# Condition lines straight to the partitions, matmuls half block diagonal, and stores from ScalarE's queue, in a conditioned residual kernel

## The reference

```
def reference(x, itok_B_1_198, L0_cond_weights):   # x (64, 64, 512), weights (200, 64, 64)
    w = weights[conditions]
    return x + einsum('bct,bcd->bdt', x, w)         # float32 throughout
```

## Time and profile before

| | us |
|---|---|
| median of 3 runs (lowest, highest) | 48.42 (48.38, 48.78) |
| the profiled execution's own time | 48.91 |
| its span | 47.0 |
| PE busy in it | 16.9 |
| VectorE busy, ScalarE busy | 13.7, 9.4 |
| bytes moved, mean rate over the span | 17.84 MB, 379 GB/s |

### The profile page before, as it was taken

The page is one execution under the profiler, slowest core; times in us unless marked ns, Lnnn a source line. Parts: engine busy times, 40 slices in busy tenths (PEclk is TensorE's granted clock), DMA queues, the critical chain, the costliest instruction groups (busy, mean ns, idle before and its releaser), DMA issues.

```text
span 47.0 us, 351 instructions
## 1 busy us (share of the span) xinstructions
PE 16.9 (36%) x128; PEld 7.0 (15%) x128; DVE 13.7 (29%) x20; ACT 9.4 (20%) x9; POOL 1.7 (4%) x9
## 2 busy tenths in 40 slices
PE   0000000000000005999999999999980000000000
PEld 0000000000000002232333554544610000000000
DVE  1006100000000893003609559559658000000000
ACT  0730000000000000003408448547647000000000
POOL 4000530000000000000000000000000000000000
PEclk9999999999999999999999999999999955555555
DMA  0679999999999999999999999999999999999800
GB/s 0 111 328 432 425 425 404 439 432 432 446 411 404 439 432 432 418 397 425 439 425 425 404 425 425 439 418 397 425 425 418 404 418 439 418 411 411 341 28 7
DMA packets 2451, 17.84 MB, mean 379 GB/s; under 512 B 274, under 2 KB 274, under 8 KB 274
## 3 DMA queue, kind: packets, MB, share of 16 engines
q1 hardware_dynamic: 2304, 16.78, 86.4%
q0 software_dynamic: 144, 1.05, 5.3%
q10 hardware_dynamic: 2, 0.00, 0.0%
HBM read 9.44 MB, written 8.39 MB: 379 GB/s over the span
## 4 chain that ended last, share of the span: by engine, by line
PE 36%; DMA 22%; issue 9%; DVE 8%; POOL 1%; POOLq 1%
PE product L110 36%; DMA gathered<-weights,table_row 22%; DVE w_all L137 5%; DVE y_sb L142 3%; POOL piece L92 1%; DVE gathered L134 1%; POOLq L29 1%; POOLq L151 0%
## 5 line engine op out<-in xcount | busy, mean ns | idle before, releaser
L110 PE MATMUL product<-x_sb,w_all 64*64 64x512 f32 x128 | 16.9, 691 | 18.1 <-DVE w_all L137 18.1
L86 ACT COPY y_sb<-product 128x1024 f32<-128x1024 f32 x8 | 8.1, 1014 | 25.2 <-PE product L110 25.2
L142 DVE COPY y_sb<-product 128x1024 f32<-128x1024 f32 x8 | 9.8, 1225 | 8.4 <-PE product L110 8.4
L110 PEld LDWEIGHTS product<-x_sb,w_all 64*64 64x64 f32 x128 | 7.0, 204 | 27.3 <-DVE w_all L137 18.1
L134 DVE TENSOR_TENSOR gathered<-gathered,piece 128x64 f32<-128x64 f32 x1 | 0.3, 270 | 10.5 <-DMA gathered<-weights,table_row 10.5
L137 DVE STREAM_TRANSPOSE w_all<-gathered 128x2048 f32<-128x2048 f32 x1 | 2.3, 2311 | 0.0
L86 ACT ACT_TABLE_LOAD x1 | 1.3, 1283 | 1.5 <-DVE condition L117 1.5
L124 DVE STREAM_TRANSPOSE condition_of<-condition 32x32 int32<-32x32 int32 x4 | 0.8, 202 | 2.5 <-DMA condition<-conditions 2.4
L94 POOL DMA_INDIRECT gathered<-weights,table_row x1 | 1.1, 1072 | 3.9 <-DVE table_row L128 3.9
L92 POOL MEMSET piece<- 32x1 f32 x4 | 0.4, 92 | 0.5 <-POOLq L151 0.3
L117 DVE MEMSET condition<- 32x64 int32 x1 | 0.1, 112 | 0.8 <-PEq L151 0.8
## 6 DMA issues: line engine op xcount, KB each, us to landing
x_sb<-x SPq DMA_DIRECT2D x8, 1024.0 KB, 14.2
out<-y_sb SPq DMA_DIRECT2D x8, 1024.0 KB, 7.1
condition<-conditions ACTq DMA_DIRECT2D x1, 0.2 KB
gathered<-weights,table_row POOLq DMA_INDIRECT x1, 10.2
```

The lines of the kernel that those rows point to most:

```text
L86: nc.scalar.copy(y_sb[:, 4 * turn:4 * turn + 2, :], product[turn % SETS][0][:, :, :]).then_inc(moved_by_act, 1)
L110: product_of = nc.tensor.matmul(product[turn % SETS][h][halves(g), j, :], w_all[halves(h), :, n], x_sb[halves(h), n, :], start=True, stop= ...
L142: nc.vector.tensor_copy(y_sb[:, 4 * turn + 2:4 * turn + 4, :], product[turn % SETS][1][:, :, :]).then_inc(moved_by_dve, 1)
```

## The change

- The conditions come as 2x32 lines of 16 integers (64 bytes), the condition first in each and zeros behind it. ScalarE loads them with two DMAs, one for each half of the partitions, and each line goes to two partitions. `condition`, its memset, the four transposes and two semaphores go; `table_row` is computed from the loaded lines.
- Turns 0 to 3 multiply as before, on quarters of the array. For turns 4 to 7 a new tensor `w_diag` holds a 128x128 matrix for each pair, with the two items' weights on the diagonal blocks and zeros beside them. VectorE and GpSimd write the zeros, ScalarE the weights: two copies of 64x256 in each of turns 0 to 3, ahead of its copy of that turn's products. A pair is then one call of 128x128 by 128x512. That is 32 calls and 16 calls, 48 instead of 64.
- ScalarE issues the stores, after its own copy and a wait for VectorE's. SyncE issues only the loads.
- The host arranges the result of the two halves differently.

```
-            for turn in range(TURNS):
-                sp.wait_ge(moved_by_act, turn + 1)
-                sp.wait_ge(moved_by_dve, turn + 1)
-                sp.dma_start(out[:, pairs_of(turn), :], y_sb[:, pairs_of(turn), :]).then_inc(stored, 16)
             sp.wait_ge(stored, 16 * TURNS)

         @block.scalar
-            act.wait_ge(condition_cleared, 1)
-            act.dma_start(condition[0:1, :], conditions).then_inc(condition_loaded, 16)
+            for h in range(PAIR):
+                act.dma_start(condition_of[halves(h), :],
+                              bass.AP(conditions.tensor, h * Q * LINE, [[0, K], [LINE, Q], [1, LINE]])
+                              ).then_inc(condition_loaded, 16)
             for turn in range(TURNS):
+                if turn < TILED:
+                    later = slice(4 * turn, 4 * turn + 4)
+                    act.wait_ge(w_ready, 1)
+                    for h in range(PAIR):
+                        nc.scalar.copy(w_diag[halves(h), later, h * D:(h + 1) * D],
+                                       w_all[halves(h), :, pairs_of(TILED + turn)].rearrange("p d n -> p n d")
+                                       ).then_inc(w_placed, 1)
                 act.wait_ge(multiplied, turn + 1)
                 nc.scalar.copy(y_sb[:, 4 * turn:4 * turn + 2, :], product[turn % SETS][0][:, :, :]
                                ).then_inc(moved_by_act, 1)
+                act.wait_ge(moved_by_act, turn + 1)
+                act.wait_ge(moved_by_dve, turn + 1)
+                act.dma_start(out[:, pairs_of(turn), :], y_sb[:, pairs_of(turn), :]).then_inc(stored, 16)

         @block.gpsimd
+            pool.wait_ge(pieces_set, 2 * (P // Q))
+            nc.gpsimd.memset(w_diag[halves(1), :, 0:D], 0.0).then_inc(w_zeroed, 1)
             pool.wait_ge(rows_known, 1)

         @block.tensor
+                if turn == TILED:
+                    pe.wait_ge(w_zeroed, 2)
+                if turn >= TILED:
+                    pe.wait_ge(w_placed, PAIR * (turn - TILED + 1))
                 for j in range(2):
                     for g in range(2):
+                        n = 4 * turn + 2 * j + g
+                        if turn >= TILED:
+                            product_of = nc.tensor.matmul(product[turn % SETS][j][:, g, :], w_diag[:, n - 4 * TILED, :],
+                                                          x_sb[:, n, :], start=True, stop=True)
+                            continue

         @block.vector
-            nc.vector.memset(condition[:, :], 0).then_inc(condition_cleared, 1)
             for q in range(P // Q):
                 nc.vector.memset(piece[q * Q:(q + 1) * Q, 1:2], float(q % K)).then_inc(pieces_set, 1)
-            dve.wait_ge(condition_loaded, 16)
-            for q in range(P // Q):
-                nc.vector.transpose(condition_of[q * Q:(q + 1) * Q, :], condition[:, q // K:B:PAIR]
-                                    ).then_inc(condition_turned, 1)
+            nc.vector.memset(w_diag[halves(0), :, D:PAIR * D], 0.0).then_inc(w_zeroed, 1)
+            dve.wait_ge(condition_loaded, 16 * PAIR)
             dve.wait_ge(pieces_set, 2 * (P // Q))
-            dve.wait_ge(condition_turned, P // Q)
...
+    conditions = np.zeros((PAIR, B // PAIR, LINE), np.int32)
+    conditions[:, :, 0] = np.asarray(itok_B_1_198).reshape(B // PAIR, PAIR).T
```

More of the change, by code:

```diff
@@ L20, in conditioned_residual_kernel @@
     P, PAIRS, T = x.shape
-    B = conditions.shape[1]
     C = D = P // PAIR
+    LINE = conditions.shape[2]
     Q = 32
@@ L44, in conditioned_residual_kernel @@
         w_all = sbuf("w_all", [P, D, PAIRS], fp32)
+        w_diag = sbuf("w_diag", [P, PAIRS - 4 * TILED, PAIR * D], fp32)
         product = [[ctx.enter_context(nc.psum_tensor(f"product{s}_{h}", [P, 2, T], fp32)) for h in range(PAIR)]
@@ L50, in conditioned_residual_kernel @@
         condition_loaded = semaphore("condition_loaded")
-        condition_cleared = semaphore("condition_cleared")
         pieces_set = semaphore("pieces_set")
-        condition_turned = semaphore("condition_turned")
         rows_known = semaphore("rows_known")
@@ L105, in _ @@
                     pe.wait_ge(moved_by_dve, turn - SETS + 1)
+                if turn == TILED:
+                    pe.wait_ge(w_zeroed, 2)
+                if turn >= TILED:
+                    pe.wait_ge(w_placed, PAIR * (turn - TILED + 1))
                 for j in range(2):
                     for g in range(2):
+                        n = 4 * turn + 2 * j + g
[3 more added lines that the diff above has]
+                            continue
                         for h in range(PAIR):
-                            n = 4 * turn + 2 * j + g
                             product_of = nc.tensor.matmul(product[turn % SETS][h][halves(g), j, :],
```

17 lines of the change are left out of this document (11 added, 6 removed).

## The result

| | before | changed |
|---|---|---|
| median, us (lowest to highest, runs) | 48.6 (48.38 to 49.01, 4) | 60.78 (60.5 to 62.15, 4) |
| profiled execution, its span | 48.91, 47.0 | 60.69, 58.7 |
| PE's start, PE's end, in the span | 18.12, 35.07 | 28.47, 53.15 |

The ratio is 1.244, 95% interval 1.233 to 1.256. The forecast was 64.4 within 56 to 67.5: the right way, and 3.6 us too much.

The account below looks back on a forecast made before the run. The prediction took DMA bytes to bound the kernel before. PE's start at 33.0 plus 30.0 behind it gave a span of 63.0; 1.9 beyond the span, less 0.5 for the median, gave 64.4 us, range 56 to 67.5.

Parts of the forecast that it names:

- The slack: At PE's start: could come 4 to 6 us later at its present pace before compute, not DMA, set the end.
- Two engines: Conditions' DMAs: the source's outermost count of 2 puts each on two engines; bounds one and sixteen.
- 66 packets, each behind a load packet.: Conditions' landing: packets per engine alternate with loads, 66 x 0.275 = 18.2 us from 2.9; wait ends at 22.6.
- From conditions to PE: Conditions' landing to first matmul: gather issued at 23.1, takes 7.2 us, lands at 30.3; PE starts at 33.0.
- Behind PE's start: PE's start to span's end: 30.0 us, with turns 0 to 3 10.1, ScalarE's delay 0.2, turns 4 to 7 13.8.
- Worth nothing: Stores on a queue apart from the loads: no gain, since the loads are over by then.
- From span to time: End of the sum: span 63.0; profiled execution 1.9 beyond its span, 64.9; median 0.5 lower, 64.4 us.
- Weight loads at nothing: PE's turns: weight loads, 16 per turn at a mean of 204 ns, hide behind streaming and cost nothing.
- The first: Rival on conditions' DMA: lines are quick, compute ends late; sixteen engines 51.0 us, or two draining many packets 49.8; chance 0.12.
- The second: Rival on conditions' DMA: each on engines of its own, or four engines; PE at 26.3, time 57.7 us; chance 0.09.
- The fourth: Rival at the start: lines drain in a burst ahead of the loads, table row at 3.3, time 48.1 us; chance 0.05.
- Profile signs: Expected in the profile: 132 small packets over some 19 us, loads landed by 24, DMA idle from 24 to 27.

Follow-up runs that it names:

- (a): Kernel before with only the conditions' lines changed (two DMAs from ScalarE, outermost count 2): 59.02 us against 48.94.
- j_tiled6_more_calls: Kernel before with the last two turns block diagonal, plus 8 small matmul calls ahead of turn 0: 50.00 us against 48.86, ratio 1.042.
- f_tiled6: Kernel before with only the last two turns block diagonal, conditions and stores as before: 47.93 us against 48.86, ratio 0.995.
- (c): Kernel before with only the stores' issue moved from SyncE to ScalarE: 48.90 us against 48.94.
- (k): Changed kernel with only the conditions as before (one line, transposes): 50.61 us against 48.38, ratio 1.045.
- (b): Kernel before with only the half block diagonal matmuls, conditions and stores as before: 49.52 us against 48.94.
- (d): Changed kernel with the conditions written out as 128 lines by the host, one DMA on sixteen engines: 50.85 us against 48.94.
- f_tiled5: Kernel before with only the last three turns block diagonal, conditions and stores as before: 48.20 us against 48.86, ratio 0.993.
- (g): Changed kernel with 128 written-out condition lines on sixteen engines and two block diagonal turns instead of four: 47.90 us against 48.38, ratio 0.989.

## Why the prediction was right, and where it was off

**What bounds the kernel.** That the bytes set the time of before held. The slack did not: PE was to start 4 to 6 us later at its present pace for nothing, but in (a) it starts 10.4 us later at that pace and the time rises by 10.1. The stores on SyncE's queue before, and then the DMA row of the page of (a), a slice being 1.43 us:

```profile
23.22 13.96 SPq L77 DMA_DIRECT2D out<-y_sb  x8
```

```profile
DMA  0799999999999999920000008999999999999910
```

Before, the first store is issued at 23.2, while the last load (landing at 25.4) still runs, and eight stores of 2.5 us follow without a gap. In (a) it is issued at 33.65: the engines run dry, and all eight end later. j_tiled6_more_calls has its first store 1.8 us later than f_tiled6 and takes some 2 us more. What has slack is the end of PE's work alone: in f_tiled6 it comes 3.1 us later than before without a loss. The prediction took the last store's slack for that of all. Its sum was not hurt, since it adds up the path behind PE's start and uses no slack.

**Two engines.** Held, by 4 closing packets in the changed kernel and by counts of 2, 4 and 128 in the experiments. The Trainium skill, "DMA: Bandwidth & Descriptors", section "Why a DMA increments its semaphore by 16 and not by 1", agrees. Its warning has the repeat as an example of a small outermost count, and count two without a repeat did the same. That the source's count would decide, and not the destination's 64, was a choice with that page's rule but no row of before behind it; it came true.

**"66 packets, each behind a load packet."** This is the step that was mis-sized. It gave 22.6 us for the end of the wait, and 17.5 was measured. In its place: a first line at 4.8 instead of 2.9 (outside its bounds of 1.8 and 3.05), then about 25 lines on each engine in a burst of 0.35 us, then 41 packets at 0.289 (11.9 us from 5.1 to 17.0; 0.275 was assumed), and 0.45 to VectorE. 4.8 + 0.35 + 11.9 + 0.45 = 17.5. I had one packet of before to go by, which can't show a burst. Late start and burst are two errors against each other: the first cost 1.9 us, the second saved some 7. The same page of the Trainium skill, section "Queues, rings and completion order", has an engine drain typically 9 to 17 descriptors in a turn, at most 64. No stretch here is of 9 to 17: the burst was of some 25 to 32 lines an engine, and happened once; after it about one line went in each turn, and on sixteen engines there was no burst.

**From conditions to PE.** Gather 7.8 us for 7.2: it met the end of the loads, where the forecast had it alone. PE's start 28.5 for 33.0, all of the difference from the conditions (-5.1) and the gather (+0.6).

**Behind PE's start.** 30.2 for 30.0, with errors that cancel, which is luck. ScalarE's small copies took 0.64 us for 0.4; the bounds were 0.25 and 1.0. The timeline of turns 3 and 4:

```profile
36.41 2.02 PE L133 MATMUL product<-x_sb,w_all 64*64 64x512 f32 x16 [0.53 <-ACT y_sb L96]
36.72 1.31 ACT L92 COPY w_diag<-w_all 64x256 f32<-64x256 f32 x2 [0.41 <-ACT y_sb L96]
...
38.05 1.01 ACT L96 COPY y_sb<-product 128x1024 f32<-128x1024 f32 x1
...
39.16 13.97 PE L129 MATMUL product<-x_sb,w_diag 128*128 128x512 f32 x32 [0.74 <-issue]
```

PE waited 0.5 us for ScalarE's copy already ahead of turn 3, and 0.7 ahead of turn 4, which begins 10.7 us behind PE's start for 10.3 forecast. Four turns took 13.99 for 13.8, the last landing 3.9 for 4.3. "Worth nothing" for the stores' queue held alone (c), not beside the small copies: (k) against (b), 0.9 us.

**From span to time.** The span was 58.7 for 63.0, 4.3 us too much, and the time only 3.6: the forecast added 1.4 us to its span, and 2.0 to 2.1 lie between the span and the time.

**Weight loads at nothing.** Held: 8 loads of 190 ns within 3.44 us of PE busy throughout, each for the whole array, and 0.86 us a call as on the quarters. The sentence of the Trainium skill that a weight load overlaps running matmuls only where row groups differ ("TensorE: Matmul & The Clock Gate", Part 3) is not what this trace shows. By it a turn would have been about 5 us, an estimate (3.44 + 8 x 0.19).

**Rivals.** The first, sixteen engines at 51.0, was (d) at 50.85 with a table row at 5.95 for 6.2. The second, four engines at 57.7, was measured at 55.1, early by the same burst. The fourth, a burst ahead of the loads, was not seen: even on sixteen engines the table row came at 5.95, not at 3.3.

**Profile signs.** Forecast: 132 small packets, as found, but over 12 us, not 19. Loads by 24: 24.3. DMA idle from 24 to 27: it idled from 25.4 on, and until the first store's packets came at 34.4, a part that the forecast did not name.

## What to carry to other kernels

Look at the outermost count of a DMA's source and destination before its bytes: 8 KB of conditions cost 10 us because an outermost 2 put all lines on two engines that were busy with loads. Count the closing packets in the page's DMA rows; they say how many engines a DMA uses. In a kernel that moves bytes all the time, look for slack at each end: here a later first store cost in full, and only later last turns cost nothing, until the engines ran dry. And a part that is free on one queue alone can cost when another part puts work behind it there.

## What the hardware showed unexpectedly

- A DMA of ScalarE on two or four engines, issued at the same moment as SyncE's loads, has its first packet at 4.8 to 4.9 us; with the loads held, at 2.1; on sixteen engines beside the same loads, at 2.2 (d). Why the start on few engines comes 2.6 us later was not found.
- Its first 50 to 64 lines on two engines, 99 on four, then pass in a burst within 0.5 us, and only the rest takes turns one by one with load packets, one in about 0.29 to 0.3 us on each engine. On sixteen engines there is no burst.
- A 16 KB instruction packet (0.93 us on one engine) shows in some executions during the stores: in (a) between 44 and 47 us, in before between 35 and 36, in f_tiled5 between 41 and 43, in (g) between 42 and 44. In all four a few packets with data trail on at the end; in f_tiled6, which has no such packet, closing packets alone are left. Whether the one causes the other is not shown, and what decides whether it comes is open. Executions of before have spans of 45.4 to 47.4.
